# Four graph layers on one core: the plain-node stage in new orders over six quads, and own rows of three attention stages split between GpSimd and ScalarE

## The reference

```python
edge_index = jnp.stack([src, dst])
h = jnp.maximum(_layernorm(x), 0.0);  x = x + _L0(h, ...)   # GCN, 128 -> 256 -> 128
h = jnp.maximum(_layernorm(x), 0.0);  x = x + _L1(h, ...)   # SAGE, two layers
h = jnp.maximum(_layernorm(x), 0.0);  x = x + _L2(h, ...)   # edge-attribute network, 3 layers
h = jnp.maximum(_layernorm(x), 0.0);  x = x + _L3(h, ...)   # attention (GAT), 4 layers, 2 heads of 64
```

## Time and profile before

| what | value |
|---|---|
| median of three runs | 5651.72 us (5638.97 to 5663.69) |
| the profiled execution | 5637.92 us, its span 5636.2 us |
| mean granted clock of TensorE | 0.897 of 2.4 GHz |
| busy share of the span | PE 72%, PE weight loads 60%, DVE 63%, ACT 47%, POOL 63% |
| DMA | 971.59 MB, mean 172 GB/s |

### The profile page before, as it was taken

One profiled execution on the slowest core, in us unless ns is written; L12 is line 12 of the kernel. 1 busy time (PEld: TensorE's weight loads), 2 busy tenths in 40 slices (PEclk: granted clock), 3 DMA queues, 4 the chain that ended last, 5 costly groups with the idle time before them and its releaser, 6 DMA issues. The chain is left out here.

```text
span 5636.2 us, 116803 instructions
## 1 busy us (share of the span) xinstructions
PE 4057.7 (72%) x27481; PEld 3359.2 (60%) x27481; DVE 3541.7 (63%) x12527; ACT 2667.5 (47%) x6624; POOL 3543.3 (63%) x4145
## 2 busy tenths in 40 slices
PE   3777777777779777988899988866676576570076
PEld 2555555555558655767788877755675575560065
DVE  5666666666666687668666669933753763676533
ACT  2555555555544343346666668832232232230086
POOL 2544545444457675767675757457777777687577
PEclk9888888888889888999999999989899899795599
DMA  2444444444445686778543436578479479579543
GB/s 72 153 151 155 151 146 155 149 157 151 148 128 149 173 227 185 208 205 248 150 119 95 118 107 175 158 224 273 111 219 283 115 189 284 146 188 394 197 133 108
DMA packets 1087196, 971.59 MB, mean 172 GB/s; under 512 B 113214, under 2 KB 845974, under 8 KB 1087036
## 3 DMA queue, kind: packets, MB, share of 16 engines
q1 hardware_dynamic: 992956, 805.13, 46.0%
q0 software_dynamic: 94080, 164.48, 12.0%
HBM read 488.42 MB, written 484.70 MB: 173 GB/s over the span
## 5 line engine op out<-in xcount | busy, mean ns | idle before, releaser
L1092 POOL DMA_INDIRECT G<-table,idx_all x1568 | 1545.9, 986 | 739.5 <-issue 499.0
L1092 POOL DMA_INDIRECT G<-table,idx_l x588 | 607.0, 1032 | 289.6 <-issue 178.0
L1042 POOL DMA_INDIRECT XIN<-in_x,idx_x x196 | 188.4, 961 | 696.3 <-ACT GN L2168 575.4
L1763 PE MATMUL PS<-ident,G 128*128 128x128 f32 x1372 | 246.2, 292 | 356.5 <-ACT G L2168 326.4
L1763 PEld LDWEIGHTS PS<-ident,G 128*128 128x128 f32 x1372 | 161.0, 146 | 471.2 <-issue 418.3
L1766 PE MATMUL PS<-G,S 128*128 (+1 forms) x2352 | 408.5, 292 | 26.3 <-DMA G<-table,idx_all 15.8
L2168 ACT ACTIVATE G<-G 128x128 f32<-128x128 f32 x784 | 323.1, 482 | 171.9 <-DVE G L1307 109.9
L1766 PE MATMUL PS<-UT,w 128*128 128x512 f32 x492 | 377.1, 911 | 13.1 <-ACT UT L2168 12.1
L1766 PE MATMUL PS<-CR,LO 97*128 97x128 f32 x2352 | 336.1, 288 | 68.1 <-ACT CR L2168 68.0
L1766 PEld LDWEIGHTS PS<-G,S 128*128 128x128 f32 x2352 | 353.8, 204 | 45.8 <-issue 28.3
L1766 PEld LDWEIGHTS PS<-S,G 128*128 128x128 f32 x1960 | 256.4, 196 | 172.8 <-issue 157.4
(11 more groups left out here) (379 smaller groups left out, 10911.0 us busy)
## 6 DMA issues: line engine op xcount, KB each, us to landing
table<-G SPq DMA_DIRECT2D x392, 256.0 KB, 2.8
table<-RO SPq DMA_DIRECT2D x271, 260.0 KB, 3.3
table<-RO SPq DMA_DIRECT2D x245, 256.0 KB
XIN<-xrows SPq DMA_DIRECT2D x196, 256.0 KB
table<-OWN SPq DMA_DIRECT2D x147, 260.0 KB, 4.0
OWN<-table SPq DMA_DIRECT2D x139, 256.0 KB, 3.3
F<-table SPq DMA_DIRECT2D x132, 256.0 KB, 3.4
S<-table SPq DMA_DIRECT2D x100, 260.0 KB
```

The costliest lines, as they stand in the source:

```text
L1042: g.indirect_dma_start(M[:, j, :], None, x, bass.IndirectOffsetOnAxis(ap=idx_x[:, t:t + 1], axis=0)).then_inc(gat[j].sem, 16)
L1092: g.indirect_dma_start(G[:, t, 0:w], None, TAB[s], bass.IndirectOffsetOnAxis(ap=idx[:, t:t + 1], axis=0)).then_inc(gat[t % 4].sem, 16)
L1763: return nc.tensor.transpose(o, i, ident[0:k, 0:k])
```

## The change

It has two parts. In the plain stage the five `plain` functions get new orders, with pieces on up to six quads (`q0` to `q5`), and `LAGS` grows from 3 to 5; two waits follow from that (`turned` for k = 3 waits for the copy of edge attributes on even quads where it did on odd ones, `attributes` waits for the quad two back, where it waited for the last), and the order of `rA` and `rB` on one semaphore is exchanged. No piece is added or left out: the same instructions stand in other places. In the GA stages POOL multiplies own rows of head 0 only; ACT multiplies head 1 with four activations per quad (Copy with a scale per partition, 128x64 each), three quads ahead, counted on a new semaphore `hself2`, for which PE waits too. ACT's GA loop is written out quad by quad in place of a hardware loop.

```diff
@@ SP: order of the body
-                load_x(q0)
-                keep(q1, "t1", q_a[1], "g", PG[1])
-                keep(q2, "t3", q_a[2], "g", PG[2])
...
+                q0, q1, q2, q3, q4, q5 = (earlier((m, 0, b), k) for k in range(6))
+                keep(q2, "t1", q_a[1], "g", PG[1])
+                next_attributes(q1)
+                keep(q4, "t3", q_a[2], "g", PG[2])
+                keep_attributes(q5)
+                keep_x(q2)
+                keep(q3, "t2", q_a[1], "t1", PR[2])
+                keep(q5, "x3", q_v[2], "xc", PX[3])
+                keep_x_norm(q3)
                 load_x(q0)
+                keep(q4, "t4", q_a[2], "rA", PR[4])
+                keep(q5, "t8", q_v[3], "r8", PR[8])
@@ DVE: order of the body
+                shift(q1, 1)
+                stats(q2, 2)
+                rows(q5, 8)
...
+                x_inverse(q1)
                 inverse(q0, 1)
...
+                stats(q3, 3)
@@ PE: order of the body
-                turned(q1, 1)
-                turned(q2, 2)
...
+                rows(q5)
+                attributes(q3)
                 turned(q1, 1)
+                rows_a(q3)
                 hidden(q1, 0)
                 hidden(q1, 1)
+                rows_b(q3)
+                convolved(q1)
+                turned(q2, 2)
+                turned(q4, 3)
                 sampled(q2)
@@ ACT: order of the body
+                rows_a(q3)
+                norm(q2, 2)
+                root(q0, 1)
+                x_root(q1)
                 turned(q2, 2)
+                turned(q4, 3)
+                convolved(q1)
                 sampled(q2)
                 norm(q0, 1)
+                turned(q0, 1)
+                root(q3, 3)
                 root(q1, 2)
+                x_norm(q1)
+                hidden(q0)
@@ POOL own_rows (GA)
-                    for h in (0, 1):
-                        oh = OWNG[n % 4][:, :, 64 * h:64 * h + 64]
-                        i = g.tensor_tensor(oh, oh, wide(PT[:, 2 + h, Q4:Q4 + 4], 64), ALU.mult)
-                    i.then_inc(hself.sem, 1)
+                    oh = OWNG[n % 4][:, :, 0:64]
+                    g.tensor_tensor(oh, oh, wide(PT[:, 2, Q4:Q4 + 4], 64), ALU.mult).then_inc(hself.sem, 1)
@@ PE sums_turned (GA)
                         pe.wait_ge(hself.sem, hself.at(s, n, "own"))
+                        pe.wait_ge(hself2.sem, hself2.at(s, n, "own"))
@@ ACT body_ga (GA)
+                    if among(n, 3):
+                        own_half(n + 3)
+
+                def own_half(n):
+                    act.wait_ge(own_g[n % 4].sem, own_g[n % 4].at(s, n // 4, "rows"))
+                    for j in range(4):
+                        row = OWNG[n % 4][:, j, 64:D]
+                        t = 4 * (LAST - n) + j
+                        i = f(row, row, ACT.Copy, scale=PT[:, 3, t:t + 1])
+                    i.then_inc(hself2.sem, 1)
```

More of the change, by code:

```diff
@@ L449, in ready @@
                 alone(eng, *waits)
-        LAGS = 3
+        LAGS = 5
         def plain_stage(eng, body):
@@ L1401, in plain @@
             def plain(m, b):
-                q0, q1, q2, q3 = (earlier((m, 0, b), k) for k in range(4))
-                inverse(q3, 3)
+                q0, q1, q2, q3, q4, q5 = (earlier((m, 0, b), k) for k in range(6))
+                shift(q1, 1)
+                stats(q2, 2)
+                rows(q5, 8)
+                aggregate(q2, 2)
+                aggregate(q4, 3)
+                x_stats(q1)
+                x_shift(q2)
+                stats(q0, 1)
                 with_bias(q1)
-                normed(q3)
-                stats(q0, 1)
+                inverse(q4, 3)
+                attributes(q3)
                 aggregate(q0, 1)
-                x_stats(q1)
+                inverse(q2, 2)
                 hidden(q1)
-                inverse(q0, 1)
[L1411 to L1425, removed]
+                shift(q2, 2)
+                residual(q3)
+                x_aggr(q1)
+                normed(q4)
+                constant(q3)
+                convolved(q1)
+                x_inverse(q1)
+                inverse(q0, 1)
+                stats(q3, 3)
             plain_stage(dve, plain)
@@ L1805, in turned @@
                 ready(pe, (free[0], earlier(q, 1), free[1]), (q_a[k], q, "half") if k < 3 else (q_v[3], q, "g"))
-                if k == 3 and q[2]:
+                if k == 3 and not q[2]:
                     alone(pe, (e_cp, turn_of(q) + 1))
@@ L1858, in attributes @@
                     return
-                ready(pe, (q_a[3], earlier(q, 1), "gT"))
+                ready(pe, (q_a[3], earlier(q, 2), "gT"))
                 alone(pe, (e_split.sem, e_split.at(0, turn_of(q), "placed")))
@@ L2246, in plain @@
             def plain(m, b):
-                q0, q1, q2, q3 = (earlier((m, 0, b), k) for k in range(4))
-                turned(q1, 1)
+                q0, q1, q2, q3, q4, q5 = (earlier((m, 0, b), k) for k in range(6))
+                rows_a(q3)
+                norm(q2, 2)
+                root(q0, 1)
+                x_root(q1)
                 turned(q2, 2)
-                hidden(q1)
+                turned(q4, 3)
+                convolved(q1)
                 sampled(q2)
-                turned(q3, 3)
-                x_norm(q2)
-                root(q0, 1)
                 norm(q0, 1)
-                convolved(q1)
-                x_root(q1)
-                rows_a(q2)
+                turned(q0, 1)
+                root(q3, 3)
                 root(q1, 2)
-                norm(q1, 2)
-                root(q2, 3)
+                x_norm(q1)
+                hidden(q0)
             act.wait_ge(pd.sem, pd.at(0, 0))
@@ L2440, in body_ga @@
                         rows_out(n - 1, 1 - h, m - 1 + h)
+                    if among(n, 3):
[7 more added lines that the diff above has]
+                    i.then_inc(hself2.sem, 1)
                 if kind == "GA":
-                    by_quads(act, body_ga, 0, 1)
+                    act.wait_ge(m_v.sem, m_v.at(0, ATTENTION.index(s), "weights"))
+                    for n in range(-3, QUADS + 1):
+                        body_ga(n, n % 2, n // 2)
                 elif kind == "C1":
```

12 lines of the change are left out of this document (2 added, 10 removed).

## The result

| | before | changed |
|---|---|---|
| median | 5646.36 us (5638.97 to 5663.69, 4 runs) | 5226.48 us (5225.34 to 5228.03, 4 runs) |
| the profiled execution, its span | 5637.92, 5636.2 us | 5226.53, 5224.8 us |
| plain stage, up to the first LO tile of C1 | 1610.1 us | 1206.9 us |
| the three GA stages, first LO tile to last | 155.0 + 162.7 + 154.9 = 472.6 us | 153.2 + 156.1 + 154.4 = 463.7 us |

The ratio is 0.9255, 95% interval 0.9244 to 0.9266. The two spans differ by 411.4 us. The plain stage gives 403.2 of it and the GA stages 8.9; the rest of the program is as long as it was in sum, within a microsecond, with single stretches up to 4 us longer or shorter. The forecast was 390 and 10. Of the 8.9, 6.7 lie in the second GA stage.

What follows compares the result with a forecast made beforehand. A ring of waits bounds the plain stage; POOL and DVE lack slack in GA. From the profiled 5637.9, less 390 (403 less 13) and 10, comes 5238; plus 13.8 to the median, 5252 us, range 5190 to 5445.

Steps and rivals of the forecast that it cites:

- the old ring: Plain stage before: each engine waits for another within one body, 15.31 us per quad; the new orders cut it.
- a ring through PE and ACT: Plain stage after: longest ring found in the new orders, once per body, 11.2 us per quad, saving 403 us.
- the crossings: Plain stage: five passages between PE and ACT at 0.19 us, 0.9 us added to the ring's 10.32.
- the gather's ring closes: Plain stage rival: POOL's gather and the chain to the norm take 25 us per two quads; 5379 us, chance 0.08.
- Filling and draining, 13: Plain stage: two more bodies of filling and draining cost between nothing and 22 us; 13 taken.
- The clock stays up: Plain stage: PE's pauses are at most about 2 us at one place, so full clock was taken.
- GA, 10 saved: GA stages: moving one of POOL's four multiplications per quad to ACT saves 10 us, between 41 saved and 21 lost.
- The 41 us: GA stages, best end: quads fall from 3.18 to DVE's 2.90 us without POOL, 41 us saved.
- The 21 us lost: GA stages, worst end: quads last 3.32 us, as when POOL was already ahead, 21 us lost.
- clock rival: Plain stage rival: the clock falls once per body as now, hidden matmuls keep 1.94 us more; 5442 us, chance 0.10.
- the slower one: Plain stage rival: the clock stays at the lower level, 18.4 us per quad; about 5950 us, chance 0.03.
- Only own work is left: Rival: crossings hide in queued work, DVE's 10.1 plus about 0.3 us sets the plain period; 5143 us, chance 0.10.

Runs made afterwards that it cites:

- e7: Changed kernel with PE's 128x512 matmul `sampled` made twice into the same bank before it is signalled; 0.9355 of the kernel before, median 5275.22 us.
- e5: Changed kernel with ACT's first half norm ahead of its relu on `sampled`, and DVE's shift for it at the body's end; 0.9177, median 5175.03 us.
- e4: Changed kernel with DVE's statistics of gathered rows moved later in the same body, to just before `residual(q3)`; 0.9213, median 5198.73 us.
- e3: Kernel before with six more 128x256 matmuls in PE's 3 us wait before each first transpose; 0.9925, median 5595.18 us.
- e8: Changed kernel with POOL's multiplication of messages in the three GA stages left out but for one column; 0.9216, median 5196.72 us.

## Why the prediction was right, and where its sum was off

- **The plain stage, 403 forecast less 13.** Measured 403. The mechanism is the one named: the old ring is cut, and a ring through PE and ACT takes its place. e7 shows it to the hundredth for `sampled`, e5 for the relu ahead of the norm: without it the body of 10.65 goes.
- **The ring's length, 11.2.** It measured 10.65. The failed term is the crossings: I added five of 0.19 to durations, 0.9, while the first half came out as summed (6.58 against 6.60) and the five steps of the second half add up to only 0.35 beyond those durations (0.64, 0.69, 1.14, 0.58 and 1.02 against 0.60, 0.58, 1.02, 0.69 and 0.83). Only four of the five cross between PE and ACT: the relu and the norm are both ACT's, and there the norm starts 0.11 before the relu's record ends. Of the four, only the one from the norm to PE costs the 0.19 that I had read; the others cost 0.04 to 0.12. Start to start on the successor, as I took `rows_a` and `convolved`, came out within 0.1.
- **The gather, costed at nothing.** With what comes up behind it, it cost 10.94 - 10.65 = 0.29 a quad, 28 us; e4 gave back 16 of them in this stage, and that much is shown to be the gather's. The rival "the gather's ring closes" had the mechanism, with 25 us for two quads, where 21.9 is what the trace shows. That the forecast of 11.2 came near the 10.94 is two errors of opposite sign.
- **Filling and draining, 13.** By the mean bodies from 300 to 1100 us, 98 x (15.33 - 10.94) = 430 would be saved at the steady pace, 403 were: 27 us, over the 22 that I gave as the most. 18 of them lie in the first 19 bodies, which take 15 us more than 19 steady ones (single bodies up to 15.4) where those of the kernel before take 3 us less. So the 403 were met by three misses that cancel: the ring 0.55 a quad too long, the gather left out, the filling too cheap.
- **The clock stays up.** Right: 1.00, the four passes 1.78 us. The longest pause in the rows is 0.74, and 0.9 in the stretch. The Trainium skill's rule on short pauses between groups of matmuls (TensorE: Matmul & The Clock Gate, "A second HAM failure mode: psum-queue depth-cycling") would have had the clock swing here; with three or four short waits in each body, the granted clock of the stretch stays 1.00. The other side: behind the 3 us of the kernel before it is 0.50 from 713 to 716 us, and in e3 it falls behind the 2.3 us.
- **GA, 10 saved.** Right in size: 9 in the profiled execution, 8 to 13 over nine. POOL is idle 30 of 100 us, waiting for loads, as said; PE's new wait shows nowhere. A quad stayed at 3.2 on the mean, not 3.1. The two ends of the range were misread, though. The 41 us took the 2.90 for every quad, and every other one, with the turn of DVE's loop, never fell under 3.11 in the traces. The 21 us lost compared a quad of 3.32 in the second stage with the 3.18 of the first; that stage's own mean was 3.39, and it is where the change gained most. The Trainium skill's rule (SBUF — State Buffer, "Who interferes with whom") that two such instructions block each other whole is near to e8: when the LO tile starts at 3652.64, POOL's product has 0.45 us to go, and the LO tile takes 0.31 longer. By the rule it would be the 0.45; the measured 0.31 is what counts.
- **The median.** The forecast for the profiled execution was 5238, measured 5226.5. The other 13.8 of the miss of 25.5 is the distance of that median from that execution, which I carried over; after the change the median lies on the profiled execution.
- **The rivals.** No clock rival came, nor the slower one. "Only own work is left" did not come either: e7's and e5's changes would have been invisible.

## What to carry to other kernels

When no engine is full, look for the ring that goes through one body of the order, and price its pieces from start to start of the successors (not durations plus a crossing each). Such a sum always closes, so it proves nothing: lengthen one piece and see whether the body grows by as much. A body without any spread is a good place to look. Then count the next ring as well, since the one that shares a queue with the first moves when the first does; an instruction that waits at the head of a queue holds up everything queued behind it. Count the turn of a hardware loop as work of the body in which it falls. Before an engine is relieved, ask whether it is the pace or only stretches the pace of another: taking a quarter of POOL's work gave 2% of a GA quad.

## What the runs showed of the hardware that was not expected

- PE with 2.6 us of matmuls for nothing in each quad made the kernel faster, by 0.75% (0.6 to 0.9), with the granted clock at 0.97 instead of 0.89 from 300 to 1100 us.
- The lower clock moves with the pause: in the same kernel sixteen passes take 2.02 us after a wait of 0.97 us and 2.68 after one of 2.33.
- In e8 a quad of GA in which DVE's hardware loop turns takes 3.12 us in two stages and 3.33 in the other, with hardly any spread; without the turn it goes down to 2.90.
- In e8 POOL's product of one column, 128x4, takes 0.20 us alone and 0.65 where it meets a DVE instruction with two inputs:

```profile
3653.05 0.65 POOL L1106 TENSOR_TENSOR G<-G,PT 128x4 f32<-128x4 f32 x1
...
3658.62 0.20 POOL L1106 TENSOR_TENSOR G<-G,PT 128x4 f32<-128x4 f32 x1
```
